# A graph network on one core: the later four steps' block products by a seven-product scheme

## The reference

```
for _ in range(5):
    s_in  = state @ in_W.T  + in_b;   a_in  = A   @ s_in
    s_out = state @ out_W.T + out_b;  a_out = A.T @ s_out
    a = concat(a_in, a_out, state)
    r = sigmoid(a @ r_W.T + r_b);  z = sigmoid(a @ z_W.T + z_b)
    h = tanh(concat(a_in, a_out, r * state) @ h_W.T + h_b)
    state = (1 - z) * state + z * h
out = tanh(state @ o1_W.T + o1_b) @ o2_W.T + o2_b
```

## Time and profile before

| | |
|---|---|
| median of 3 runs | 1374.04 us (1374.02 to 1374.37) |
| profiled execution, span | 1372.5 us, some 1.5 us below the median of the runs |
| PE busy | 1354.4 us, 99% of the span |
| DVE busy | 464.9 us, 34% |
| ACT busy | 224.5 us, 16% |
| mean granted TensorE clock | 0.997 of full speed |
| DMA | 33.4 MB, nearly all in the first eighth of the span |

### The profile page before, as it was taken

One profiled execution on the slowest core, in us unless ns is written; L12 is line 12 of the kernel. 1 busy time (PEld: TensorE's weight loads), 2 busy tenths in 40 slices (PEclk: granted clock), 3 DMA queues, 4 the chain that ended last, 5 costly groups with the idle time before them and its releaser, 6 DMA issues.

```text
span 1372.5 us, 14932 instructions
## 1 busy us (share of the span) xinstructions
PE 1354.4 (99%) x5322; PEld 654.9 (48%) x5322; DVE 464.9 (34%) x882; ACT 224.5 (16%) x439; POOL 3.0 (0%) x9
## 2 busy tenths in 40 slices
PE   7999999999999999999999999999999999999998
PEld 5666544444444444444444444444444444444445
DVE  6577732314142230423224032322413323141225
ACT  4756110101121010111101011110101101010011
POOL 0000000000000000000000000000000000000000
PEclk9999999999999999999999999999999999999999
DMA  8454200000000000000000000000000000000021
GB/s 280 154 169 139 85 0 0 0 0 1 0 1 0 0 0 0 0 0 0 0 0 0 0 0 0 0 0 0 0 0 0 0 0 0 0 0 0 0 80 62
DMA packets 16796, 33.40 MB, mean 24 GB/s; under 512 B 1025, under 2 KB 6402, under 8 KB 16386
## 3 DMA queue, kind: packets, MB, share of 16 engines
q1 hardware_dynamic: 15760, 29.23, 6.5%
q0 software_dynamic: 720, 3.67, 0.7%
q10 hardware_dynamic: 290, 0.14, 0.0%
HBM read 27.27 MB, written 5.77 MB: 24 GB/s over the span
## 4 chain that ended last, share of the span: by engine, by line
PE 90%; DVE 0%; issue 0%; ACT 0%; DVEq 0%
PE bank L205 88%; PE bank L398 1%; PE bank L321 0%; DVE H L738 0%; PE bank L274 0%; DVE DR L706 0%; DVE AT L695 0%; DVE A L877 0%; DVE stat L645 0%; PE bank L294 0%; ACT H L493 0%; DVE nrm L672 0%; DVE nrm L671 0%; DVE nrm L670 0%; DVE nrm L669 0%
## 5 line engine op out<-in xcount | busy, mean ns | idle before, releaser
L205 PE MATMUL bank<-work,WG 128*128 128x512 f32 x1120 | 485.9, 592 | 0.0
L205 PE MATMUL bank<-AT,SN 128*128 (+1 forms) x1280 | 485.1, 379 | 0.0
L205 PE MATMUL bank<-A,SN 128*128 (+1 forms) x1280 | 485.1, 379 | 0.0
L205 PEld LDWEIGHTS bank<-work,WG 128*128 128x128 f32 x1120 | 211.9, 190 | 262.1 <-issue 262.1
L833 DVE SCALAR_TENSOR_TENSOR work<-DR,gcol,bank 128x512 f32<-128x512 f16 x120 | 89.7, 748 | 394.4 <-PE bank L205 394.0
L205 PEld LDWEIGHTS bank<-A,SN 128*128 (+1 forms) x1280 | 125.2, 98 | 154.3 <-issue 6.3
L205 PEld LDWEIGHTS bank<-AT,SN 128*128 (+1 forms) x1280 | 125.2, 98 | 152.3 <-issue 4.5
L610 ACT ACTIVATE work<-work,col 128x512 f32<-128x512 f32 x120 | 86.6, 722 | 549.1 <-DVE work L837 549.1
L808 DVE TENSOR_SCALAR work<-bank 128x512 f32<-128x512 f32 x40 | 25.8, 686 | 385.8 <-PE bank L205 385.8
L205 PE MATMUL bank<-ST,WG 128*128 128x512 f32 x320 | 140.6, 592 | 0.0
L205 PEld LDWEIGHTS bank<-ST,WG 128*128 128x128 f32 x320 | 60.8, 190 | 69.8 <-issue 67.0
(11 more groups left out here) (80 smaller groups left out, 489.8 us busy)
## 6 DMA issues: line engine op xcount, KB each, us to landing
WG<-in_adj SPq DMA_DIRECT2D x32, 512.0 KB, 4.7
SN<-in_x SPq DMA_DIRECT2D x2, 1024.0 KB, 10.7
x_d<-SN POOLq DMA_DIRECT2D x4, 512.0 KB, 2.9
A<-x_d SPq DMA_DIRECT2D x1, 2048.0 KB, 8.2
out<-A SPq DMA_DIRECT2D x4, 512.0 KB, 2.9
A<-in_wg_t SPq DMA_DIRECT2D x2, 768.0 KB, 6.2
fused_d<-AT POOLq DMA_DIRECT2D x1, 1536.0 KB, 6.4
WG<-fused_d SPq DMA_DIRECT2D x1, 1536.0 KB, 6.9
```

The lines of the kernel that those rows point to most:

```text
L205: return pe.matmul(o, l, r, start=start, stop=stop)
```

## The change

The first step is computed as before. In the other four the target nodes are taken in two halves of 1024 (`n % 2`, so `n` runs over 8 half steps), and per half two sums (x = 0 with `AT`, x = 1 with `A`) are each a two by two block product: features in two halves of 128, inner nodes in two sets of eight tiles, target nodes in two blocks of 512. It is formed from seven block products (M1 to M7) in place of eight, with sums of blocks on the left (`LF`, seven float16 pairs made from the turned state by ACT and DVE: `leaf`, `leaf_first`, `leaf_sums`, `leaf_low`) and on the right (`quad_d`). A block product is 16 float16 matmuls (8 tiles, high and low part). The gate products on those sums are done likewise, with seven float32 pairs of matmuls (`W7`, X11 to X22, XT2 to XT4) in place of eight pairs; the products on the state itself stay plain.

The right blocks and their sums are made once: after block 1 of step 1 DVE makes eight sums of 128 x 4096 float16 (`quad_sums(0)`), after block 2 eight more (`quad_sums(1)`). SP writes all 28 blocks of 1 MB to DRAM (`quad_d`), then loads 12 pieces of gate weights (`W7`), and then streams 112 blocks of 1 MB back through six slots. The slots, `LF`, `W7` and the X buffers lie where `A`, `AT`, `SN` and `work` were. All steps are written out, without loops. The scale 1/2^11 goes into the folded weights. The three last loads on SP now wait for the last block product.

```diff
+            for p in range(2):
+                for y, m in ((0, AT), (1, A)):
+                    for op, c, half in ((M1, 2 * p, 0), (M2, 2 * p, 1), (M3, 2 * p + 1, 1)):
+                        sp.dma_start(quad_d[y, p, op]..., quad(m, c, half)).then_inc(quads_out, 16)
...
+            for k in range(14 * 2 * (STEPS - 1)):
+                n, y, i = k // 14, k // 7 % 2, k % 7
+                if k == 4:
+                    sp.wait_ge(sums_out[2], 16 * 4)
+                if k >= SLOTS:
+                    o = k - SLOTS
+                    sp.wait_ge(prod_ready, 7 * (o // 7) + place(o // 14, o // 7 % 2, LOADS[o % 7]) + 1)
+                sp.dma_start(slot[k % SLOTS][:, :, :], quad_d[y, n % 2, LOADS[i]]).then_inc(ld_slot[k % SLOTS], 16)
...
+            def product(n, x, op, o, k0, k1):
+                k = 14 * n + 7 * x + LOADS.index(op)
+                b = slot[k % SLOTS]
+                if k0 == 0:
+                    pe.wait_ge(ld_slot[k % SLOTS], 16 * (k // SLOTS + 1))
+                for t in range(k0, k1):
+                    for h in range(2):
+                        last = mm(o[:, :], LF[:, op, t, h, :], b[:, t, :],
+                                  t == 0 and h == 0 and op in (M1, M5, M6),
+                                  t == HALF - 1 and h == 1, True)
+                if k1 == HALF:
+                    last.then_inc(prod_ready, 1)
...
+                part(M1, a, True).then_inc(part_ready, 1)
+                part(M5, c, True).then_inc(part_ready, 1)
+                part(M6, b, True).then_inc(part_ready, 1)
...
+                pe.wait_ge(part_act, 2 * done + 1)
+                part(M2, a, False)
+                own(0, n1, (0, 3), a, False).then_inc(part_ready, 1)
+                pe.wait_ge(part_act, 2 * done + 2)
+                part(M3, c, False)
+                own(0, n2, (1, 2), c, False).then_inc(part_ready, 1)
+                pe.wait_ge(part_dve, PARTS * done + AT_U2)
+                part(M7, b, True).then_inc(part_ready, 1)
+                own(1, n2, (1, 2), d, True).then_inc(part_ready, 1)
+                pe.wait_ge(part_dve, PARTS * done + AT_U3)
+                part(M4, b, False)
+                own(1, n1, (0, 3), b, False).then_inc(part_ready, 1)
...
+            for b in range(NB):
+                if b > 0:
+                    spread(b, 0, NT).then_inc(agg_done, 1)
+                gates(b)
+            for n in range(2 * (STEPS - 1)):
+                for x in range(2):
+                    products(n, x)
+                for j in range(3):
+                    gate_group(n, j, n // 2 == STEPS - 2)
...
+            def quad_sums(p):
+                for x, m in ((0, AT), (1, A)):
...
+                    v.tensor_tensor(t1, b12, b11, ALU.subtract).then_inc(quad_sum, 1)
+                    v.tensor_tensor(t2, b22, t1, ALU.subtract).then_inc(quad_sum, 1)
+                    v.tensor_tensor(t3, t2, b11, ALU.subtract).then_inc(quad_sum, 1)
+                    v.tensor_tensor(t4, b21, t2, ALU.subtract).then_inc(quad_sum, 1)
...
+            for b in range(NB):
+                first_step(b)
+                if b == 1:
+                    dve.wait_ge(quads_out, 16 * 12)
+                    quad_sums(0)
+                if b == 2:
+                    dve.wait_ge(sums_out[0], 16 * 8)
+                    quad_sums(1)
```

More of the change, by code:

```diff
@@ L22 @@
 STEPS = 5
+HALF = NT // 2
+M1, M2, M3, M4, M5, M6, M7 = range(7)
+PLAIN = (M1, M6, M5, M2, M7, M3, M4)
+EARLY = (M1, M2, M6, M5, M7, M3, M4)
+LOADS = (M1, M6, M5, M2, M7, M3, M4)
+SLOTS = 6
+PARTS, AT_U2, AT_U3 = 10, 3, 9
 SCALE = 2.0 ** 11
@@ L154, in graph_net, with quad, half_banks, place @@
         block = ctx.enter_context(nc.Block())
+        def quad(m, c, half):
+            return m[:, c, :, :].rearrange("p (u h q) n -> p u h (q n)", u=2, h=2)[:, :, half, :]
+        def half_banks(g):
+            return bank[4 * (g % 2):4 * (g % 2) + 4]
+        def place(n, x, op):
+            return (EARLY if n % 2 == 0 and x == 0 else PLAIN).index(op)
+        def act_place(n, x, what):
+            return (("m1", "c11", "m5") if n % 2 == 0 and x == 0 else ("m1", "m5", "c11")).index(what)
+        def leaf_tiles(p):
+            return [(f, BT * (2 * p + h) + q) for f in range(2) for h in range(2) for q in range(BT)]
         @block.sync
@@ L378, in gates @@
                     last.then_inc(gate_ready, 1)
[L379 to L384, removed]
+                    if b == NB - 1 and t in (1, 2):
+                        pe.wait_ge(state_ready, 4)
+                        for op in (("L11", "L12"), ("L22", "L21"))[t - 1]:
+                            leaf(0, op, bank[("L11", "L12", "L22", "L21").index(op)])
+                pe.wait_ge(gate_dve, 6 * b + 2)
                 for t in (4, 5):
@@ L507, in convert @@
                 t = BT * b + 2 * h + r
-                copy(A[:, t, c * 512:c * 512 + 512], ring[:, k % RING, r, :],
+                copy(A[:, c, t, :], ring[:, k % RING, r, :],
                      accum_out=degA[:, t, c:c + 1]).then_inc(conv, 1)
@@ L585, in _, with out_pq @@
                 stage()
-            def out_pq(g):
-                act.wait_ge(agg_done, g + 1)
+            def out_pq(b):
+                act.wait_ge(agg_done, b + 1)
                 for f in range(FT):
[L591 to L615, removed]
@@ L617, in _, with leaf_first @@
-            with act.Fori(0, STEPS - 1) as s:
-                step(s, False)
-            step(STEPS - 1, True)
+                    copy(PQ[:, f, :], bank[f][:, :]).then_inc(pq_act, 1)
+            def leaf_first(i, order, banks):
+                p, k0 = i % 2, BT * (i % 2)
+                for op in order:
+                    at_op = ("L11", "L12", "L22").index(op)
+                    act.wait_ge(leaf_ready, 4 * i + at_op + 1)
+                    act.wait_ge(leaf_lo, 7 * i)
+                    o = banks[op][:, :].rearrange("p (q n) -> p q n", q=BT)
+                    copy(fresh[op][:, :, :], o).then_inc(leaf_act, 1)
+                    copy(LF[:, (M1, M2, M4)[at_op], k0:k0 + BT, 0, :], o, SCALE).then_inc(leaf_hi, 1)
@@ new lines, in gate_group @@
+            def gate_group(n, j, last_step):
+                p = n % 2
+                g = 5 * n + 2 + j
+                a, b, c, d = half_banks(g)
+                done = 3 * n + j
+                buf = gate_buf[j]
+                act.wait_ge(part_ready, 8 * done + 1)
+                copy(temp[:, g % 2, 0, :], a[:, :]).then_inc(part_act, 1)
+                act.wait_ge(part_ready, 8 * done + 2)
+                copy(buf[:, 2, :], c[:, :]).then_inc(part_act, 1)
+                fresh_here = j == 0 and p == 1 and not last_step
+                if fresh_here:
+                    other = half_banks(g - 1)
+                    leaf_first(n + 1, ("L11", "L12", "L22"), dict(zip(("L11", "L12", "L22"), other)))
+                for i, tile in enumerate((0, 1, 2, 3)):
+                    act.wait_ge(value_ready, 12 * n + 4 * j + i + 1)
+                    f = (0, 0, 1, 1)[i]
+                    nc.scalar.activation(buf[:, tile, :], buf[:, tile, :], ACT.Tanh if j == 2 else ACT.Sigmoid,
+                                         bias=col[:, 10 + 2 * j + f:11 + 2 * j + f]).then_inc(squashed, 1)
+                    if fresh_here and i == 1:
+                        leaf_sums(n + 1)
+                    if i == 1 and j == 2 and p == 1 and not last_step:
+                        leaf_first(n + 2, ("L11",), {"L11": a})
@@ new lines, in _ @@
+            for b in range(NB):
+                if b > 0:
+                    act.wait_ge(state_ready, 2 * b)
+                out_pq(b)
+                for t in range(6):
+                    act.wait_ge(gate_dve, 6 * b + t + 1)
+                    v = (RS, Z, cand)[t // 2][:, t % 2, :]
+                    nc.scalar.activation(v, v, ACT.Tanh if t >= 4 else ACT.Sigmoid,
+                                         bias=col[:, 10 + t:11 + t]).then_inc(gate_act, 1)
+                    if b == NB - 1 and t == 2:
+                        act.wait_ge(quad_sum, 16)
+                        act.wait_ge(quads_out, 16 * 12)
+                        leaf_first(0, ("L11", "L12", "L22"),
+                                   dict(zip(("L11", "L12", "L22"), bank[0:3])))
+                    if b == NB - 1 and t == 3:
+                        leaf_sums(0)
@@ new lines, in _, with leaf_low @@
+            LEAVES = (("L11", M1), ("L12", M2), ("L22", M4), ("S2", M6), ("S1", M5), ("S3", M7), ("S4", M3))
+            def leaf_low(i, first, end):
+                k0 = BT * (i % 2)
+                for e in range(first, end):
+                    op, m = LEAVES[e]
+                    dve.wait_ge(leaf_hi, 7 * i + e + 1)
+                    if e < 3:
+                        dve.wait_ge(leaf_act, 3 * i + e + 1)
+                    elif e in (4, 5, 6):
+                        dve.wait_ge(leaf_sum, 4 * i + 4)
+                    else:
+                        dve.wait_ge(leaf_sum, 4 * i + 2)
```

(18 more changed lines are left out.)

584 lines of the change are left out of this document (450 added, 134 removed).

## The result

The changed kernel takes 1287.57 us (median of 4 runs, 1285.99 to 1288.11) against 1374.2 us: a ratio of 0.9366, 95% interval 0.9353 to 0.938. The forecast was 1288. The profiled execution has a span of 1284.2 us.

The account below looks back on a forecast made before the run. PE's matmuls, count times pace, were taken as the bound. 1372.5 - 96.4 + 0 + 6.6 + 2 + 2 + 0 = 1286.7 us; with the median 1.5 us above the span, 1288 us, range 1281 to 1308.

Parts of the forecast that it names:

- Bound and paces: Step before the change: PE-bound, 237.6 us from matmuls at 0.2158 (float16) and 0.858 us (float32) plus transposes.
- What goes, 96.4 us: Later four steps: 256 fewer float16 matmuls (55.2 us) and 48 fewer float32 matmuls (41.2 us) on PE.
- The sums in step 1, 0 us: DVE's float16 sums, about 2.5 us each, hide before PE needs the copy behind them; upper end 17 us.
- rival 1: Step 1's float16 sums run at one element a cycle: plus 17 us, 1305 us; chance 0.12.
- From step 1 to step 2, 6.6 us: PE idles once, waiting for block 3's last state update; bounds 5.8 and 9 us.
- The left sums' 0.8: End of step 1: DVE's left sums ahead of the last two biases add about 0.8 us to PE's idle time.
- The clock, 2 us: Behind the idle gap after step 1 the granted clock may fall: 2 us, between 0 and 3.4.
- Handoffs, 2 us: Later steps' gate groups: all PE waits for DVE and ACT results together 2 us, from 0 to 16.
- rival 2: PE loses a late operation in every gate group: plus 16 less the 2 taken, 1302 us; chance 0.14.
- The stream, 0 us: Slot loads in later half steps may take 4.8 us each, were expected at 2.6, so cost nothing.
- Rival 3: Slot stream can't keep up: even at 6.1 us a load; at 7.9 plus 198, 1486 us; chance 0.04.
- Sum: Whole kernel: terms give a 1286.7 us span; median 1.5 us above it, so 1288 us; chance 0.65.

Follow-up runs that it names:

- s9: Changed kernel with plain gate products (24 float32 matmuls a group, not 22), matmuls on the first sum's X placed before PE's wait: 1327.8 us, ratio 0.9659.
- s1: Changed kernel with step 1's sixteen float16 sums issued as scalar_tensor_tensor in place of tensor_tensor: 1307.28 us.
- s10: The changed kernel itself, unedited, in a second set of runs: 1286.19 us, ratio 0.9359 to the kernel before.
- s4: Changed kernel with 26 float16 matmuls into a dead bank while PE waits for step 1's last state update: 1284.78 us, ratio 0.9342.
- s6: Changed kernel with four unused DVE reductions of 512 elements ahead of U3 in each half step's third gate group: 1300.06 us.
- s3: Changed kernel with one extra 1 MB DRAM to DRAM copy behind each of the 112 slot loads: 1298.9 us.
- s8: Changed kernel with two extra 1 MB DRAM to DRAM copies behind each slot load: 1476.34 us, ratio 1.0724.
- s5: Changed kernel with first halves of M1, M6 and M5 run before PE's wait for the last state update in step 2's first half step: 1280.42 us.
- s7: Changed kernel with gate products back to eight plain pairs (24 float32 matmuls a group, not 22), adjacency products kept at seven: 1337.68 us.
- s2: Changed kernel with three slots in place of six for the streamed blocks: 1312.51 us.

## Why the prediction was right, step by step

- **Bound and paces.** Right. One step's stretch was taken apart into two paces and a count with nothing left over, and the same paces give the new step: 213.5 forecast, 213.49 measured. The float16 matmuls kept theirs under 295 GB/s of DMA.
- **What goes, 96.4 us.** Right: 96.5. s9 shows the gates' share by itself, 10.30 of the 24.12 us a step.
- **The sums in step 1, 0 us.** Right. One took 2.28 to 2.29 us; the ratio from the one-tensor form said 2.5. The table of the Trainium skill (VectorE: DVE Perf Modes, The perf-mode tier table) has such a sum at twice the float32 pace; the estimate from it was 2.3, and the trace agrees. s1 shows what hung on it: 21 us, more than the 17 that rival 1 was given, because the clock's loss behind a wait was left out of its price.
- **From step 1 to step 2, 6.6 us.** 5.7 measured. The left sums' 0.8 didn't appear: ACT and DVE were through at 389.8, just before the bias at 390.14.
- **The clock, 2 us.** 2.6 in this profile and 1.4 in that of s10, for the same gap; s4 has none of it. The warning of the Trainium skill (TensorE: Matmul & The Clock Gate, Why this matters for your kernels) of a gap between bursts held: here the fall followed 5.7 us of idle PE, which no row of before had shown.
- **Handoffs, 2 us.** 0: PE shows no such wait in any of the 24 groups. U3 was made at 929.84 and wanted at 930.45, a margin of 0.6 us where 0.3 was reckoned. s6 puts it at 0.7: with more than that added to DVE's work in front of U3, rival 2 comes true.
- **The stream, 0 us.** Right, and s3 (4.9 us, 1.4 us of waits a half step) and s8 (7.7 us) show the threshold near 4.8 us and the price beyond it. Rival 3's break-even of 6.1 us was not measured; the sum by pitch that it rests on gave 186 of 190 us in s8, with the clock's loss inside it.
- **Sum.** 1372.5 - 96.5 + 5.7 + 2.6 is 1284.3; the span is 1284.2. The start was 0.6 us shorter (the first weights' load, 6.0 for 6.6 us), which is chance and leaves 0.5 us unexplained. The forecast's 1286.7 was 2.5 too long by the 2 for handoffs and 0.9 of the gap, less 0.6 of clock. That the median came within half a microsecond was luck: the profiled run was the fastest of its four, and the others were 1 to 2 us longer, which the forecast had no term for. Their mean clock was lower (0.993 for 0.994), and s10's profile shows such a loss in the first part, which the change leaves alone.

## What to carry to other kernels

If one stage's length is a count times a pace with nothing left, a change of the count can be priced to the microsecond, provided each helper engine and each transfer is checked for the moment at which its result is wanted, not for its mean load. Write that moment down for each: 27.4 us for eight sums, 4.8 us for a load, 15.5 us for U3. And look at what the new order can't overlap at its seams: the one gap that the change made could be filled by the halves that were ready (s5).

## What the hardware showed beside it

A wait of PE can cost more than its own length. Waits of 1.5 us on average (s6) and of 0.83 us (s7) cost 1.7 and 1.07, and the granted clock stayed at 1.00 around them. Waits of 3.07 to 3.21 (s2), 5.7 (the changed kernel) and 7.7 us (s1) were each followed by some microseconds at the 1.2 GHz level, 1.4 to 3.0 us of work more. For one and the same gap of 5.7 us that loss was 1.4 us in s10 and 2.6 in the first profile, so it is a range and not a price. In s8 it came to 50 of 190 us. A copy from DRAM to DRAM behind each load took no more DMA time than a load: 428 GB/s with copies, 402 GB/s in the earlier trace rows without.
